# Graph layer with top-2 experts: more row and result buffers in the expert stage, scatters further behind gathers, last groups loaded ahead of stores

## The reference, cut to what matters

```python
xn = _layernorm(x, axis=-1)
x = x + _L0_gnn_ref(xn, edge_weight, src, dst) + _L0_mix_ref(xn[None], ...)[0]
x = x + _L0_ffn_ref(_layernorm(x, axis=-1)[None], router_w, w1, b1, w2, b2)[0]

# inside _L0_ffn_ref: tokens is the normalised x, E = 8, TOP_K = 2
out = tokens
for e in range(E):
    h = jax.nn.gelu(tokens @ w1[e] + b1[e], approximate=False)
    y = h @ w2[e] + b2[e]
    out = out + combine[:, e:e + 1] * y
```

## Time and profile before

| what | us |
|---|---|
| median of three runs | 2375.53 (2367.39 to 2375.83) |
| the profiled execution | 2373.04 |
| its span | 2371.3 |
| PE busy (matmuls) | 2089.1 (88%) |
| PE busy loading weights | 1795.3 (76%) |
| DVE busy | 1478.1 (62%) |
| POOL busy | 1410.8 (59%) |
| ACT busy | 1168.3 (49%) |

### The profile page before, as it was taken

One profiled execution on the slowest core, in us unless ns is written; L12 is line 12 of the kernel. 1 busy time (PEld: TensorE's weight loads), 2 busy tenths in 40 slices (PEclk: granted clock), 3 DMA queues, 4 the chain that ended last, 5 costly groups with the idle time before them and its releaser, 6 DMA issues. The chain is left out here.

```text
span 2371.3 us, 36271 instructions
## 1 busy us (share of the span) xinstructions
PE 2089.1 (88%) x11864; PEld 1795.3 (76%) x11864; DVE 1478.1 (62%) x2689; ACT 1168.3 (49%) x3503; POOL 1410.8 (59%) x1282
## 2 busy tenths in 40 slices
PE   5888689998999899989998999899999974988885
PEld 3576578987898789878987898789889963766664
DVE  6784477758775777577758775877467767010112
ACT  5530154565456545554565455545566640443332
POOL 1001677667766776677667766776666621666663
PEclk9898899999999999999999999999999985999897
DMA  7523732232223222322232223222333331566667
GB/s 251 171 66 117 238 103 83 83 93 78 84 85 89 81 80 84 93 81 81 81 93 81 83 83 92 82 83 83 88 113 115 115 91 32 171 196 191 209 213 232
DMA packets 157568, 270.84 MB, mean 114 GB/s; under 512 B 28309, under 2 KB 105124, under 8 KB 157384
## 3 DMA queue, kind: packets, MB, share of 16 engines
q0 software_dynamic: 59584, 161.78, 23.0%
q1 hardware_dynamic: 62796, 72.81, 9.5%
q10 hardware_dynamic: 35004, 33.93, 4.8%
HBM read 223.61 MB, written 45.77 MB: 114 GB/s over the span
## 5 line engine op out<-in xcount | busy, mean ns | idle before, releaser
L1154 POOL DMA_INDIRECT edge_G<-xn_scratch,edge_row_i x1029 | 1156.1, 1123 | 485.8 <-issue 252.6
L1254 ACT ACTIVATE edge_weighted<-edge_hots,bins_scale 128x128 f32<-128x128 bf16 x2401 | 738.7, 391 | 52.8 <-DVE edge_row_hots L1311 52.8
L1221 PE MATMUL edge_op<-edge_win,edge_A 128*128 128x256 f32 x2744 | 667.9, 387 | 63.2 <-issue 41.0
L1221 PEld LDWEIGHTS edge_op<-edge_win,edge_A 128*128 128x128 f32 x2744 | 528.6, 194 | 148.7 <-issue 48.7
L1245 ACT COPY edge_A<-edge_ap 128x512 f32<-128x512 f32 x343 | 200.8, 585 | 722.8 <-PE edge_ap L1204 554.3
L1217 PE MATMUL edge_op<-edge_G,edge_weighted 128*128 128x256 f32 x2058 | 509.2, 383 | 19.8 <-DVE all_xn L1324 17.2
L1306 DVE TENSOR_TENSOR edge_hots<-bins_iota128b,bins_recb 128x1024 bf16<-128x1024 bf16 x343 | 237.3, 692 | 381.3 <-PE edge_ap L1204 292.8
L1217 PEld LDWEIGHTS edge_op<-edge_G,edge_weighted 128*128 128x128 f32 x2058 | 365.2, 191 | 62.8 <-DVE all_xn L1324 20.7
L1204 PEld LDWEIGHTS edge_ap<-edge_weighted,edge_row_hots 128*128 128x128 f32 x2744 | 360.9, 194 | 47.7 <-DMA edge_win<-xn_scratch 13.8
L1204 PE MATMUL edge_ap<-edge_weighted,edge_row_hots 128*128 128x128 f32 x2744 | 370.7, 279 | 14.8 <-DMA edge_win<-xn_scratch 13.4
L1311 DVE TENSOR_TENSOR edge_row_hots<-all_iota,bins_recd 128x512 f32<-128x512 f32 x343 | 239.1, 697 | 0.0
(11 more groups left out here) (291 smaller groups left out, 1853.0 us busy)
## 6 DMA issues: line engine op xcount, KB each, us to landing
exp_w1x<-in_w ACTq DMA_DIRECT2D x105, 256.0 KB
edge_G<-xn_scratch,edge_row_i POOLq DMA_INDIRECT x1029
exp_ys<-ys_scratch SPq DMA_DIRECT2D x12, 1024.0 KB
ln_xin<-in_x SPq DMA_DIRECT2D x12, 512.0 KB, 5.5
xn_scratch<-ln_xnb ACTq DMA_DIRECT2D x12, 512.0 KB, 6.5
xnT_scratch<-ln_xT SPq DMA_DIRECT2D x12, 512.0 KB, 6.9
mix_xg<-xn_scratch SPq DMA_DIRECT2D x12, 512.0 KB, 3.9
mix_ek<-xnT_scratch SPq DMA_DIRECT2D x12, 512.0 KB, 4.8
```

The source lines that it names most:

```text
L1154: pool.indirect_dma_start(out=G[:, t % AHEAD, i, :], out_offset=None, in_=xn_dram, in_offset=bass.IndirectOffsetOnAxis(ap=row_i[:, q % 2, ...
L1221: last = nc.tensor.matmul(op[j][:, :], A[:, j, i, :], win[:, q % 2 * DN + i, :], start=False, stop=i == DN - 1)
L1254: last = nc.scalar.activation(weighted[:, t % 2, i, :], hots[:, t % 2, i // 2, :, i % 2], ACT.Copy, scale=scale[:, b, i:i + 1])
```

## The change

In the expert stage `XB`, the number of buffers for gathered rows, goes from 4 to 6; the buffers of `w1` get a number of their own, `WB` = 4; `YB`, the number of result buffers, goes from 4 to 8, and so does the number of counters that SP reads for each group; `AHEAD` goes from 7 to 10; `CBUF` goes from 4 to 3. SP takes the counts of the last group from constants, and the store of group 9 stands behind the last two loads instead of between them. In the first stage the semaphore `eps_set` goes, and its one increment is made on `stats_done`, whose waits are raised by one; `expert_block` needs more semaphores than before.

```diff
--- before.py
+++ after.py
@@ -493,7 +493,6 @@
         x_in = [st.sem(f"x_in{j}") for j in range(XB)]
         xn_out = [st.sem(f"xn_out{j}") for j in range(XB)]
         xT_out = [st.sem(f"xT_out{j}") for j in range(TB)]
-        eps_set = st.sem("eps_set")
         stats_done = st.sem("stats_done")
         shift_done = st.sem("shift_done")
         xn_act = st.sem("xn_act")
@@ -547,7 +546,7 @@
 
             @block.vector
             def _(dve):
-                nc.vector.memset(eps[:, :], EPS).then_inc(eps_set, 1)
+                nc.vector.memset(eps[:, :], EPS).then_inc(stats_done, 1)
                 bins.dve_consts(dve)
 
                 def greatest(g):
@@ -563,7 +562,7 @@
                     for s in range(n):
                         last = nc.vector.bn_stats(stats[:r, j, s, :], xin[:r, j, s, :])
                     last.then_inc(stats_done, 1)
-                    dve.wait_ge(stats_done, g + 1)
+                    dve.wait_ge(stats_done, g + 2)
                     if g >= XB:
                         dve.wait_ge(std_done, g - XB + 1)
                     for s in range(n):
@@ -637,7 +636,7 @@
 
             @block.scalar
             def _(act):
-                act.wait_ge(eps_set, 1)
+                act.wait_ge(stats_done, 1)
                 act.wait_ge(w_in, 32)
 
                 def root(g):
@@ -1924,15 +1923,16 @@
                  out, ident):
 
 
-    AHEAD = 7
+    AHEAD = 10
     DOWN = 3
-    XB = 4
-    YB = 4
-    CBUF = 4
+    XB = 6
+    WB = 4
+    YB = 8
+    CBUF = 3
     G1 = NG + 1
     with Stage(nc, "exp") as st:
         xt = st.sb("xt", [P, XB, D])
-        w1x = st.sb("w1x", [P, XB, KC, D])
+        w1x = st.sb("w1x", [P, WB, KC, D])
         xT = st.sb("xT", [P, 2, KC, P])
         gT = st.sb("gT", [P, DOWN, KC, P])
         yt = st.sb("yt", [P, YB, D])
@@ -1951,7 +1951,7 @@
         up = [[st.ps(f"up{j}{f}", [P, P]) for f in range(KC)] for j in range(2)]
         dn = [st.ps(f"dn{j}", [P, D]) for j in range(2)]
         x_in = [st.sem(f"x_in{j}") for j in range(XB)]
-        w1_in = [st.sem(f"w1_in{j}") for j in range(XB)]
+        w1_in = [st.sem(f"w1_in{j}") for j in range(WB)]
         y_out = [st.sem(f"y_out{j}") for j in range(YB)]
         c = st.sem("c")
         pe_c = st.sem("pe_c")
@@ -1985,6 +1985,8 @@
                 LATE = 2
 
                 def counts_of(g):
+                    if g == G1 - 1:
+                        return [16 * len(range(k, NXT, YB)) for k in range(YB)]
                     return [sp.value_load(tiles_i[0:1, k, g:g + 1], min_val=16, max_val=16 * (NXT // YB + 1))
                             for k in range(YB)]
 
@@ -2009,9 +2011,9 @@
                     load(g, counts)
                     if g + 1 < G1:
                         counts = counts_of(g + 1)
-                    if g >= LATE:
+                    if g >= LATE and g < G1 - 2:
                         store(g - LATE)
-                for g in range(G1 - LATE, G1):
+                for g in range(G1 - 2 - LATE, G1):
                     store(g)
                 for k in range(YB):
                     sp.wait_ge(y_out[k], 16 * len(range(k, NXT, YB)))
@@ -2060,13 +2062,13 @@
                         last.then_inc(t1_done, 1)
                     if live(i, 1):
                         t = i - 1
-                        pe.wait_ge(w1_in[t % XB], 16 * (t // XB + 1))
+                        pe.wait_ge(w1_in[t % WB], 16 * (t // WB + 1))
                         pe.wait_ge(xT_done, t + 1)
                         if t >= 2:
                             pe.wait_ge(gT_done, 2 * t - 2)
                         for f in range(KC):
                             for k in range(KC):
-                                last = nc.tensor.matmul(up[t % 2][f][:, :], w1x[:, t % XB, k, f * P:(f + 1) * P],
+                                last = nc.tensor.matmul(up[t % 2][f][:, :], w1x[:, t % WB, k, f * P:(f + 1) * P],
                                                         xT[:, t % 2, k, :], start=k == 0, stop=k == KC - 1)
                             last.then_inc(up_done, 1)
                     if live(i, DOWN):
@@ -2089,9 +2091,9 @@
 
                 def load_w1(t):
                     number_of[t] = expert_of(act, t)
-                    act.dma_start(w1x[:, t % XB, :, :],
+                    act.dma_start(w1x[:, t % WB, :, :],
                                   w1[bass.ds(number_of[t], 1), :, :].rearrange("a (c p) f -> p (a c) f", p=P))\
-                        .then_inc(w1_in[t % XB], 16)
+                        .then_inc(w1_in[t % WB], 16)
 
                 for t in range(2):
                     load_w1(t)
@@ -2150,7 +2152,7 @@
                     last = v.tensor_scalar_add(tiles_i[:, k, :], tiles_f[:, :], float(YB - 1 - k))
                 link(last)
                 flat = tiles_i[:, :, :].rearrange("p k g -> p (k g)")
-                link(v.tensor_single_scalar(flat, flat, 2, op=ALU.arith_shift_right))
+                link(v.tensor_single_scalar(flat, flat, 3, op=ALU.arith_shift_right))
                 link(v.tensor_single_scalar(flat, flat, 4, op=ALU.logical_shift_left))
                 dve.sem_inc(counted, 1)
                 for g, rows in enumerate(ROWS):
```

## The result

The changed kernel took **2354.77 us** in the median of 6 runs (2349.19 to 2359.53), beside 2372.16 us for the kernel before (6 runs, 2367.39 to 2375.83): ratio **0.9931**, 95% interval 0.9915 to 0.9948, 17.4 us less. The forecast was 35 us less (2338 against 2373). The direction and the wait that was to go held, the size was half.

What follows compares the result with a forecast made beforehand. The prediction took POOL's waits for ACT's copies, late because PE's completions are held, to bound the expert stage. Sum: 2373.0 - 38 (stage) + 5 (clock) - 2 (tail) = 2338 us; eight-in-ten range 2310 to 2377.

Steps and rivals of the forecast that it cites:

- The binding wait: Expert stage, POOL: scatters waiting for ACT's copy (69.8 us in 33 waits) give way to gathers waiting for a transpose.
- The pause: POOL's stop in the expert stage after a run of DMAs: 1.1 us forecast, for 2.2 to 2.4 us before.
- 38 x 0.8 = 30 us: POOL's new waits of gathers for transposes in the expert stage: 38 stops, each 0.8 us over the fixed 0.30.
- the 8 us for the last ten scatters: End of the expert stage: POOL's last ten scatters wait for results one by one, 0.8 us each on average.
- Clock, 5 us given back: PE in the expert stage: two or three tiles at the slower granted clock stay uncovered, 5 us lost, bounds 0 and 20.
- Tail, 2 us less: End of the program: load 12 issued earlier, so the last sum and last store come 2.0 us sooner.
- w1 next in line: Expert stage: w1 loads, kept at four buffers, may be waited for next; 0 to 10 us, 0 in the sum.
- No change: Rival, chance 0.17: PE's work really takes 3.2 us a tile, or ACT's chain needs the long stop; 2371 us.
- The pace comes to the w1 loads or the DMA engines: Rival for the expert stage, chance 0.10: these loads or engines set 3.0 us a tile, 22 us gained, 2349 us.
- POOL stops pausing: Rival for the expert stage, chance 0.10: enough completions slip out between DMAs, 68 us go, about 2305 us.
- Slower: Rival for the expert stage, chance 0.10: PE gets one tile per POOL stop, 3.4 us a tile, 20 us more, 2391.
- The base reading: Expert stage: back-to-back indirect DMAs on POOL hold PE's completions; a POOL stop of about 1 us lets them out.

## Why the prediction was half right

- **The binding wait moves from ACT's copy to the transposes: right.** 69.8 us in 33 waits became 9.9 in 6, and 41 waits on `exp_t` came (38 forecast, "30 to 45"), 47 with the six marked "remote".
- **The pause is 1.1 us instead of 2.2 to 2.4: right.** The mean is 45.1 / 41 = 1.10 us.
- **The term that failed is "0.8 us over the fixed 0.30", in "38 x 0.8 = 30 us" and in the 8 us for the last ten scatters.** The 57.2 us of fixed gaps (29.0 + 28.2) were taken as if they held 0.30 us for each of the 210 instructions. They are the gaps of those that did not wait. An instruction that waits has its 0.30 inside its wait, so about 48 instructions had to be charged 1.1 us, not 0.8. On the old side of the sum the waits stood at full length (76.3 us), on the new one at the shortened, which made a gain out of nothing. With the terms put right: 267.4 + 38 x 1.1 + 10 x 1.1 = 320.2 us, 23.5 less than 343.7; measured 323.8, 19.9 less. All of POOL's waits after are 62.5 us in 55, where the sum had 38 us. The whole sum would have been 2373.0 - 23.5 + 5 - 2 = 2352.5 us, for 2354.8 in the median; the 2349.2 profiled hold 5.1 us of luck from the stages ahead.
- **Clock, 5 us given back.** The clock rose from 0.91 to 0.95 and not near 1, so slow stretches remain. The prediction took PE to be idle for under 1 us at a time; it still stood for up to 2.1 us. With the corrected terms the stage would be 18.5 us shorter, for 19.9; the 5 us are of the right order, and not measured by themselves.
- **Tail, 2 us less: wrong.** 1.17 us more. The bound named for it, store 9 as the thing waited for, is what the row shows (1.22 us before the last sum); taking the wait away gave 1.3 us back. The eight register loads were also taken too lightly, at 0.5 us that the last scatter would cover: store 8 comes 5.48 us behind its load instead of 2.74, and load 11 goes out 1.47 us later behind the last scatter. (The last store runs for 4.6 us, from 2366.7 to the span's end at 2371.3, and not for the 3.9 us written; no term hangs on that.)
- **Row buffers.** The prediction credits "six gathered-row buffers, scatters ten behind" together. The runs part them: the buffers give nothing, and each takes one tile from the distance, so that of the three tiles added one was needed for the gain and two to pay for the two buffers more.
- **Eight result buffers at nothing: right** (0.9940 with four, 0.9931 with eight).
- **w1 next in line: right, small.** 8.3 us in 5 waits of PE, and 17.3 us once the scatters are gone.
- **Rivals.** "No change" falls: PE runs a tile in 2.38 us with plain transfers on POOL. "The pace comes to the w1 loads or the DMA engines" had the better number, 22 us gained, and the stage is at 322.8 / 105 = 3.07 us a tile, near its 3.0; but its reason is not in the rows: PE waits 8.3 us for w1, the DMA share is 0.67, and it is 0.76 and 0.80 in the faster stages with plain transfers. The rule weighed there (Trainium skill, Perfetto Trace Analysis, section Tensor Engine Instruction), that a matmul's end is computed and its semaphore follows PSUM, agrees with the trace in so far as a matmul's recorded end does not tell when others see it: ACT starts 0.03 us later in the run with plain transfers, 5.0 us later beside indirect ones. The rule gives neither number, and the slow PE that I had derived from it is not there. "POOL stops pausing" falls: completions do not trickle out in its stead. "Slower" falls: 105 tiles with 47 such stops are 2.2 tiles per stop, not under 1.3.
- **The base reading**, that PE's completions are held while POOL issues indirect transfers back to back, stood as inferred. The two runs with plain transfers bear it out, one with POOL busy for 113 of 287 us and one with 256 of 287. What the mechanism inside the chip is stays open, also whether PE's signals wait or the last step of its matmuls does.

## What to carry to other kernels

When engines are coupled by buffer counts and an issue distance, write down which tile's result each wait needs when the neighbouring wait has just been met: here one digit (AHEAD 8 for 7) was worth all of a change with three deeper sets of buffers, and more row buffers raised the distance needed. In a sum over an engine's account, an idle time before an instruction is either a fixed gap or a wait; when waits are shortened, count the new one at its full length, since its fixed gap lies inside it. When a transfer is moved to another engine's queue, add its issue to that engine's cycle: the 0.35 us of a store made ACT the slowest here. And where POOL issues indirect transfers in a row, look in the trace for late signals of PE (up to 5.0 us here), and for what can be stored or loaded in plain form.

## What the runs showed of the hardware

- Beside back-to-back indirect transfers on POOL, ACT got to see a matmul of PE 5.0 us after its end in the cycle quoted of the changed kernel (3.7 us in the one of the kernel before), each time 1.1 to 1.2 us after POOL's last transfer ended. With plain transfers and memsets that keep POOL busy without a gap, it is 0.03 to 0.04 us. In the cycle quoted, ACT's own signal reached PE within 0.10 us. The time of the whole program differs by 2% (ratios 0.9931 and 0.9734).
- A plain transfer of 128 KB keeps POOL for 0.54 us, an indirect one for 0.98 to 1.02 us plus 0.30 us before the next.
- A memset of 128x768 on POOL took 0.76 us.
- A plain store issued from ACT's queue in each tile (0.35 us) brought ACT's cycle to 2.62 us, over the 2.38 us of PE.
